# Last stage: the additions to the residual on GpSimd wait for the last router product, and SyncE stores all normalised rows first

## The reference

```python
weights = (jnp.einsum('bsd,do->bso', x, wr) + br)[..., 0]
k = max(1, int(CAPACITY * s))
kk = k - 1 if k > 1 else 1
_, idx = jax.lax.top_k(weights, k)
sel_idx = idx[:, :kk]
sel = jnp.take_along_axis(x, sel_idx[:, :, None], axis=1)
h = jax.nn.gelu(jnp.einsum('bkd,dh->bkh', sel, w1) + b1)
y = jnp.einsum('bkh,hd->bkd', h, w2) + b2
y = y * w_sel[..., None]
processed = jnp.zeros_like(x).at[batch_idx, sel_idx].set(y)
return processed + x
```

## Time and profile before

| | |
|---|---|
| median of 3 runs | 5131.09 us (5129.94 to 5133.36) |
| the profiled execution's own time | 5129.8 us |
| its span, first to last instruction | 5128.1 us |
| mean granted TensorE clock | 0.941 of full speed |
| busy: PE, DVE, ACT, POOL | 82%, 66%, 27%, 49% |
| last stage in this execution | about 4810 us to the end |

### The profile page before, as it was taken

How to read it: one execution, slowest core, us unless ns; L and a number is a source line. 1 busy time by engine, 2 the same in 40 slices (tenths; PEclk the granted TensorE clock), 3 DMA queues, 4 the chain that set the end, 5 groups by cost and what they waited for, 6 DMA issues and landing times. The chain is left out here.

```text
span 5128.1 us, 77007 instructions
## 1 busy us (share of the span) xinstructions
PE 4200.7 (82%) x20133; PEld 3514.9 (69%) x20134; DVE 3366.2 (66%) x8997; ACT 1359.9 (27%) x4238; POOL 2535.6 (49%) x2647
## 2 busy tenths in 40 slices
PE   6787877777777999999866999999288888888359
PEld 3486655665656888988755888888166666666258
DVE  8987877877777777777675111111778777786841
ACT  5385000000044444444263222222200000002512
POOL 0002777777725777777601222222257777774221
PEclk8898999999999999999998999999589999999779
DMA  3201333333323333333412222211723333332620
GB/s 94 46 1 33 105 105 104 105 104 104 105 62 109 106 106 106 106 106 106 132 44 98 70 78 93 93 52 44 228 81 104 104 104 104 104 104 81 203 60 19
DMA packets 250615, 476.19 MB, mean 93 GB/s; under 512 B 61052, under 2 KB 155053, under 8 KB 250422
## 3 DMA queue, kind: packets, MB, share of 16 engines
q0 software_dynamic: 126848, 345.69, 23.3%
q1 hardware_dynamic: 118374, 123.01, 7.7%
q10 hardware_dynamic: 5200, 5.24, 0.3%
HBM read 490.23 MB, written 69.36 MB: 109 GB/s over the span
## 5 line engine op out<-in xcount | busy, mean ns | idle before, releaser
L1064 PE MATMUL sum_sums<-sum_got,sum_onehot 128*128 x9408 | 2193.3, 388 | 426.6 <-SPq L114 293.8
L1064 PEld LDWEIGHTS sum_sums<-sum_got,sum_onehot 128*128 128x128 f32 x9408 | 1774.8, 192 | 807.4 <-issue 574.1
L997 POOL DMA_INDIRECT sum_got<-xn,edge_row x1568 | 1496.1, 954 | 1068.9 <-DVE edge_row L1094 544.7
L1276 DVE TENSOR_TENSOR acc<-acc,sum_sums 128x256 f32 (+1 forms) x2352 | 990.8, 421 | 602.9 <-PE sum_sums L1064 342.4
L997 POOL DMA_INDIRECT sum_got<-h,edge_row x784 | 741.1, 945 | 349.1 <-issue 238.5
L789 ACT ACTIVATE xb<-xb,edge_weight 128x98 f32<-128x98 f32 x1568 | 430.9, 363 | 509.0 <-DVE xb L759 507.8
L2082 DVE TENSOR_TENSOR moe_f_y<-moe_f_ps_y,moe_b 128x256 f32<-128x256 f32 x112 | 42.3, 420 | 670.5 <-PE moe_f_ps_y L2026 670.5
L1222 DVE TENSOR_SCALAR sum_onehot<-iota,sum_now 128x128 f32<-128x128 f32 x1584 | 425.8, 362 | 7.5
L1232 DVE TENSOR_SCALAR sum_onehot<-iota,sum_now,ones 128x128 f32<-128x128 f32 x1584 | 424.3, 368 | 7.1
L2011 PE MATMUL moe_f_ps_h<-moe_f_xT,xb 128*128 128x256 f32 x1792 | 424.7, 380 | 0.0
L2026 PE MATMUL moe_f_ps_y<-xb,moe_f_hT 128*128 128x256 f32 x1792 | 422.7, 379 | 0.0
(11 more groups left out here) (508 smaller groups left out, 3925.0 us busy)
## 6 DMA issues: line engine op xcount, KB each, us to landing
xb<-in_L_ffn_W SPq DMA_DIRECT2D x112, 1024.0 KB
sum_got<-xn,edge_row POOLq DMA_INDIRECT x1568, 2.7
xn<-xb SPq DMA_DIRECT2D x21, 896.0 KB, 4.1
sum_got<-h,edge_row POOLq DMA_INDIRECT x784, 2.7
moe_out_c_got<-moe_rows SPq DMA_DIRECT2D x49, 256.0 KB, 3.1
h<-xb SPq DMA_DIRECT2D x7, 896.0 KB, 4.2
x<-acc SPq DMA_DIRECT2D x7, 896.0 KB
pair<-xb SPq DMA_DIRECT2D x7, 896.0 KB
```

The costliest lines, as they stand in the source:

```text
L997: pool.indirect_dma_start(got[:, c % SU, 0:D], None, source, bass.IndirectOffsetOnAxis(ap=p.edge_row[:, c:c + 1], axis=0)).then_inc(s_got[ ...
L1064: mm = nc.tensor.matmul(sums[k % 2][j], onehot[:, ((k % 2) * HALF + j) * PAIR + r, :], pair[:, r, :], start=(r == 0), stop=(r == PAIR - 1))
L1276: v.tensor_tensor(a, a, sums[k % 2][j], ALU.add).then_inc(s_added[j], 1)
```

## The change

On GpSimd the seven waits for ScalarE's rows are replaced by one wait ahead of the first addition: all 49 router products must be through (which implies that all rows have been written). On SyncE the loop is cut in two: first all seven stores of normalised rows, then for each step the two stores of the sums.

```diff
             @block.gpsimd
             def _(pool):
+                pool.wait_ge(s_dots, NT)
                 for i in range(STEPS):
-                    pool.wait_ge(norm.s_by_act, U * i + U)
                     own = p.acc[:, U * i:U * i + U, 0:D]
                     nc.gpsimd.tensor_tensor(own, own, p.xb[:, U * i:U * i + U, :], ALU.add).then_inc(s_base, 1)
...
                     t = slice(U * i, U * i + U)
                     sp.wait_ge(norm.s_by_act, U * i + U)
                     sp.dma_start(x_dram[:, t, :], p.xb[:, t, :]).then_inc(s_kept, 16)
+                for i in range(STEPS):
+                    t = slice(U * i, U * i + U)
                     sp.wait_ge(s_base, i + 1)
                     sp.dma_start(base_dram[:, t, :], p.acc[:, t, 0:D]).then_inc(s_kept, 16)
                     if i < STEPS - 1:
```

## The result

| | before | after |
|---|---|---|
| median | 5131.24 us (20 runs) | 5138.26 us (20 runs) |
| ratio | | 1.0014, 95% interval 1.0007 to 1.002 |
| profiled execution: own time, span | 5129.8, 5128.1 | 5138.64, 5136.9 |

The change made the kernel 7.0 us slower, 0.14%; the forecast was 7.0 slower, "same" by the bound of 0.2%. The interval does not contain 1.0, so the kernel did become slower, and its upper end lies on that bound.

What follows compares the result with a forecast made beforehand. The first block was taken as held by SyncE issuing stores; its exit would move from 4867.37 to 4874.4, so 5129.8 + 7.0 = 5136.8, with the median 1.3 above: 5138.1 us, range 5132 to 5142.

Steps and rivals of the forecast that it cites:

- step 1: First block, VectorE: undisturbed products end at 4837.4 instead of 4860.24; the 22.9 us gained all become waiting at L2099.
- step 2: First block, GpSimd: seven additions at 3.79 us each run 4837.4 to 4863.9; by itself the wait would cost nothing.
- First sum stored: First block: the first addition is done at 4841.2 instead of 4817.8, its store then ending the queue's gap.
- step 4: SyncE's queue: 12.82 MB stand behind the first sum and move at 342 GB/s, 5.37 us per pair of stores.
- step 5: First block's exit: SyncE is through after 11.01 MB, at 4874.4 against 4867.37, 7.0 us later.
- all but the last 1.81 MB: First block's exit: SyncE's last issue ends with the last three stores, 1.81 MB, still to be moved.
- step 6: Second block: the last store lands at about 4882, hidden beside the search; it would decide only from 54 us later.
- step 7: PE's clock near the first FFN matmuls: its rise may shift against them by +-1.5 us, taken as 0.
- stores at 384: Rival, SyncE's queue: stores move 384 GB/s, exit at 4870.9, +3.5 us, 5134.6; chance 9%.
- stores slower than 311: Rival, traffic from 4841 to the exit: below 311 GB/s the exit comes 10.3 us later; at 300, 5142.6; chance 7%.
- The 317 of the earlier trace: Another stage's stretch with row stores in pieces: 317 GB/s taken as slow bound, exit 4876.9, +9.5 us.
- The products' gain at the end of the program: Rival: the exit does not wait for SyncE, so the search starts 22.9 us sooner, 5108.2; chance 3%.

Runs made afterwards that it cites:

- e1: The kernel before with only GpSimd's wait for the last router product added, SyncE's order unchanged; 5156.39 us against 5131.92, ratio 1.0048.
- e7: The kernel before with the two weight loads issued in the second block; one run, 5131.58 us against 5130.75 for before.
- e2: The kernel after with GpSimd's old waits restored, SyncE's new order kept; 5134.92 us against 5131.92 for before, ratio 1.0007.
- e6: Against e3, sums made on ScalarE in the second block and stored from there, no GpSimd additions; 5104.27 us against 5130.75 for before, ratio 0.9948.
- e3: The kernel after with SyncE's stores of the sums issued in the second block; 5127.46 us against 5131.92 for before, ratio 0.9993.

## Why the prediction was right

Point by point, in its own steps, in us from the start of the rows:

- *Products* (step 1): last one at 27.0 predicted, 27.2 measured. All of the gain did turn into waiting at L2099.
- *Additions* (step 2): 3.79 each taken, between 3.37 and 3.88; measured 25.41 / 7 = 3.63. They ended at 52.7 (53.5 predicted). As the step said, they are not what sets the pace: with stores at 5.4 us a pair, the 0.16 us each made no difference. The step's sentence that the wait by itself would cost nothing holds for GpSimd's own end only: in e1, with SyncE's old order, it moved the exit by 23.6 us, because the stores of rows 2 to 7 then stood behind the first sum.
- *First sum stored* at 30.8 predicted, 31.1 measured (4843.73 - 4812.62).
- *Rate* (step 4): 342 taken; 341, 338 and 344 in the three stretches after. The rate was right, but the ground for leaving out 384 was not: that was no mixture with loads still moving (see e7). What held is that the stores ahead of the exit run at the rate that they had shown in the kernel before from 4834 on; what sets the one rate or the other stays open.
- *Exit* (step 5): SyncE through at 64.0 predicted (4874.4 - 4810.43), 64.4 measured. The rule with which it was reckoned, all but the last 1.81 MB, also held in e1 (80.5 and 80.55) and e2 (60.3 and 60.19), where the bytes behind the first sum, or the moment of that first store, were others; in e7 it missed by 1.3.
- *Landing* (step 6): hidden. In e6, with 16 us to spare, it still is.
- *Clock and the rest* (step 7): the part from the first gather on was 0.8 us shorter in the profiled execution, within the 1.5 allowed. What moves it by up to 2.8 us between executions was not tested. It goes with the clock: counted from the first gather, the granted clock is 1.00 (2.4 GHz) from 11 us on in e3, where this part took 196.0, from 13 in the kernel after, 14 in the kernel before, and 15 in e6, where it took 198.7.

The rivals: stores at 384 and stores slower than 311 both fell with the 338 to 344 of the kernel after, with GpSimd adding or not. The 317 of the earlier trace rows was no rate of a full queue: one store starts inside that stretch (DMA share 0.94), and where that stage's queue is full it moves 345 to 350. The products' gain at the end of the program fell with 37.44 us of idling at the exit. Its price was also too small in the prediction: from the search's start at 57.5 to the products' end at 27.2 it is 30 us, not 22.9; in e6, where the exit comes with the products, it came 28.9 sooner. That the 7.0 us of the forecast and of the medians agree to a tenth is luck: in the profiled pair the exit came 7.5 later, and the executions differ by 8.8, of which 2.2 arose before this stage.

## What to carry to other kernels

When all engines meet at the end of a block, find the engine that arrives last before freeing one that arrives early; here that was a queue of stores, on an engine that does no arithmetic. For such a queue, count the bytes that stand behind the moment when it can first run without a gap, and divide by the rate that its own kind of traffic shows; work put in a row ahead of that moment delays all of them. Two engines that lock each other out are not helped by putting them in a row when both must be through: give the work to a third that stands idle, and let the stores run beside the next block.

## What was not expected of the hardware

- Behind two loads that had landed, stores of 1 KB rows moved 383 GB/s for 13 us; from 4834 on, in the kernel after behind the first sum, and without loads ahead (e7) they moved 338 to 349 over stretches of 5 us and more. Taking 2.10 MB of loads out of the first block did not shorten it (56.9 and 57.0).
- VectorE's instructions with one SBUF tensor, on 49 int32 values per partition, were held up by GpSimd's additions as long as the router product with its two (3.4 to 3.6 us instead of 0.19).
